# The waits of a three-bank PSUM ring rewritten, and two of its rounds moved to another phase, in a fused attention and mixture-of-experts kernel

## The chip, the cores and the metric

One core of a Trainium2 chip. The metric is the device time of one launch in microseconds (us), lower is better. Before the change it is 879.34 us, the median of three runs (878.54 to 879.36).

## What is computed

Two blocks, one after the other, in fp32 on `x` of 2 x 1024 rows of 256. Cut to what matters:

```python
# q from the layer-normed x (1024 rows), keys and values from 64 context rows and the same 1024 rows
q, k, v = map(to_heads, (q, k, v))            # 8 heads of 64, per batch of 2
q = l2norm(q) * q_scale
k = l2norm(k) * k_scale
sim = jnp.einsum('bhid,bhjd->bhij', q, k) * SCALE
sim = jnp.where(full_mask, sim, max_neg)      # the mask is over the 64 context keys
attn = jax.nn.softmax(sim.astype(jnp.float32), axis=-1)
out = jnp.einsum('bhij,bhjd->bhid', attn, v)
x = x + layer_norm(out @ Wo, ln_o_w, ln_o_b)
...
x = x + shared_swiglu(h) + top2_of_16_experts(h)   # h = layernorm(x)
```

The change touches the attention alone.

## The kernel before

**Stages.** Projections come first (to about 114 us), then attention, `stage_b(i)` for `PAIRS = 8` pairs `i` of one batch entry and two heads (114 to about 514 us), then the output projection, the shared experts and the routed experts. Each engine's program is written out by hand, and semaphores tie them; nothing is scheduled by a tool.

**A pair.** There are 1024 queries in `CH = 2` halves of 512, and `TK = 9` key tiles of 128. A *slot* (`score_slot`, L798 to L824) is one key tile against one half for both heads: three products (`L814`) and one that adds the negated row maxima (`L823`), eight matmuls into two of the banks 0 to 3. ScalarE turns each bank into `prob` (`exponentials`, L1145 to L1160, one instruction a head). A pair has 18 slots, in six *phases* `f` of three. After its three slots a phase *weighs* the three `prob` of the phase before, six matmuls (12 with both passes of fp32) into bank 7 (`weigh`, L826 to L842). In phases 0 and 3 a `total` (L844 to L850) follows: the row sums of one half, from `acc`, which GpSimd adds up out of `prob` (L634, L639). The last three `prob` of a half are added on VectorE (`add_tail`, L1401 to L1409) and put onto `acc` by GpSimd (L645).

**The maxima of the next pair.** While pair `i` runs, TensorE transposes the rows of pair `i+1` (`turn_heads`, phases 0 and 1) and makes 17 *rounds* (`piece_round`, L755 to L782). A round is one query tile against one half of the keys, two matmuls, one a head (`L768`); round 16 is the masked context keys (`L774`, `L779`, 18 small matmuls). VectorE reduces each of the two banks to row maxima (`reduce_round`, `L1361`, `L1364`), and after round 16 `negate` (`L1370`, `L1374`) makes `zneg`. The next pair's first matmul (`turn_neg`, `L788`) transposes it, and VectorE spreads it (`keep_neg`, `L1379`).

**Where a round stands.** `ROUNDS[f]` has four places: ahead of the phase's first slot, and behind each of its three slots. VectorE goes through the same lists, place by place (`stage_b`, L1456 on). In phase 3 it does `add_tail` first; in phases 2 and 5 a `divide` (`L1426`, it needs `rec`, which comes back by DMA) stands behind the rounds, and in phase 5 ahead of `negate`. Pair 0 makes its own rounds and those of pair 1 by other lists (`FIRST_ROUNDS`), which the change leaves alone, and pair 7 makes none.

**The ring.** Turns, rounds, `neg` and `sum` all write banks 4, 5, 6 in turn: use `u` of the list `ring_order` takes bank `4 + u % RING`, `RING = 3`, and must wait until use `u - 3` has been read. VectorE counts `ring_used` up for each of them but the sums, ScalarE counts `sum_kept` for the sums (`keep_sum`, L1162 to L1167). `ring_freed(n)` and `ring_kept(n)` are the two counts after `n` uses. Both heads of a round wait ahead of the round's first matmul:

```python
        def ring_slot(*key):

            u = ring_at[key]
            if u >= RING:
                wait(pe, ring_used, ring_freed(u + 1 - RING))
                wait(pe, sum_kept, ring_kept(u + 1 - RING))
            return ring_bank(u)
...
            two = [ring_slot("piece", i, r, h) for h in range(2)]
```

Round 13 of pair 1, as one of the others, has two: first the `ring_used` of its second head, then both `sum_kept`, and the matmul carries the `ring_used` of its first head.

Of the kernel before, what the change touches and what calls it, by code (L numbers as in the profile page):

```python
# [60 lines left out]
RING = 3  # L61
# [7 lines left out]
def wait(eng, sem, value):  # L69

    if isinstance(value, int) and value <= 0:
        return
    eng.wait_ge(sem, value)

def build(nc, x, ctx, mask, ln_x_w, ln_x_b, ln_l_w, ln_l_b, wq, wkv, q_scale, k_scale, wo,
# [6 lines left out]
    def sem(name):  # L83
        return es.enter_context(nc.semaphore(name))
# [143 lines left out]
    ring_made, ring_used, hi_ready = sem("ring_made"), sem("ring_used"), sem("hi_ready")  # L228
# [3 lines left out]
    sum_kept, o_kept, sum_spread = sem("sum_kept"), sem("o_kept"), sem("sum_spread")  # L232
# [31 lines left out]
    def slot_loop(eng, body):  # L264
# [6 lines left out]
        for s in range(NS // 4 * 4, NS + 1):  # L271
# [3 lines left out]
    MASKED_ROUND = CH * TQ  # L275
    K_LEFT, Q_LEFT, K_RIGHT, K_CTX, Q_RIGHT = range(TURNS)
    TURN_AT = {0: (K_LEFT, Q_LEFT), 1: (K_RIGHT, K_CTX, Q_RIGHT)}
    ROUNDS = {1: ((), (0,), (1,), (2,)), 2: ((3,), (4,), (5,), (6,)), 3: ((7,), (8,), (9,), (10,)),
              4: ((11,), (12,), (13,), (14,)), 5: ((15,), (16,), (), ())}

    HALF = TQ // CH
    LATE_MASKED = MASKED_ROUND + 1
# [15 lines left out]
    def phase_rounds(i, f):  # L298
# [3 lines left out]
        if i + 1 == PAIRS:  # L302
            return [()] * (BATCH + 1)
        return [[(i + 1, r) for r in place] for place in ROUNDS.get(f, ((),) * (BATCH + 1))]

    def masked_tiles(i, r):

        if i == 0:
            return {MASKED_ROUND: (0, HALF), LATE_MASKED: (HALF, TQ)}.get(r)
        return (0, TQ) if r == MASKED_ROUND else None  # L310
# [7 lines left out]
    ring_at, ring_order = {}, []  # L318
# [33 lines left out]
    def ring_freed(n):  # L352

        return sum(key[0] != "sum" for key in ring_order[:n])

    def ring_kept(n):

        return sum(key[0] == "sum" for key in ring_order[:max(n, 0)])

    def ring_bank(u):  # L360

        return bank[4 + u % RING]
# [324 lines left out]
    def _(pe):  # L687
# [46 lines left out]
        def ring_slot(*key):  # L734

            u = ring_at[key]
            if u >= RING:
                wait(pe, ring_used, ring_freed(u + 1 - RING))
                wait(pe, sum_kept, ring_kept(u + 1 - RING))
            return ring_bank(u)  # L740

        def turn_heads(i, g):

            b, j = divmod(i, PAIRS // B)
            cols = slice(j * P, (j + 1) * P)
            if g == K_CTX and b == 1 and j == 0:
                pe.wait_ge(k_used, NT + B)
            src, first, n = {K_LEFT: (kn, 0, 4), K_RIGHT: (kn, 4, 4), K_CTX: (kn, TQ, 1),
                             Q_LEFT: (on, 0, 4), Q_RIGHT: (on, 4, 4)}[g]
            dst = ring_slot("turn", i, g)  # L750
            for a in range(n):
                last = nc.tensor.transpose(dst[:, a * P:(a + 1) * P], src[:, first + a, b, cols], ident[:, :])  # L752
            last.then_inc(ring_made, 1)

        def piece_round(i, r):  # L755

            p, b = i % 2, i // (PAIRS // B)
            two = [ring_slot("piece", i, r, h) for h in range(2)]
            if masked_tiles(i, r) is None:
                t, c = divmod(r, CH)  # L760
                if r == 0:
                    pe.wait_ge(ring_used, ring_freed(ring_at[("turn", i, Q_LEFT)] + 1))
                if r == 1:
                    pe.wait_ge(ring_used, ring_freed(ring_at[("turn", i, K_RIGHT)] + 1))
                if t == TQ // 2 and c == 0:
                    pe.wait_ge(ring_used, ring_freed(ring_at[("turn", i, Q_RIGHT)] + 1))
                for h, rows in enumerate((LOW, HIGH)):
                    mm_(two[h][:, :], q_hi[p][rows, t * P:(t + 1) * P], k_hi[p][rows, c * QC:(c + 1) * QC],  # L768
                        start=True, stop=True).then_inc(ring_made, 1)
            else:  # L770
                t0, t1 = masked_tiles(i, r)
                pe.wait_ge(ring_used, ring_freed(ring_at[("turn", i, K_CTX if t1 <= TQ // 2 else Q_RIGHT)] + 1))
                for h, rows in enumerate((LOW, HIGH)):
                    mm_(two[h][:, 0:(t1 - t0) * M].rearrange("p (t m) -> p t m", m=M), firstrow[rows, :],  # L774
                        maskrow[rows, b, :].unsqueeze(1).to_broadcast([DH, t1 - t0, M]),
                        start=True, stop=False, skip_group_check=True)
                for t in range(t0, t1):
                    for h, rows in enumerate((LOW, HIGH)):
                        last = mm_(two[h][:, (t - t0) * M:(t - t0 + 1) * M], q_hi[p][rows, t * P:(t + 1) * P],  # L779
                                   k_hi[p][rows, S:S + M], start=False, stop=(t == t1 - 1), skip_group_check=True)  # L780
                        if t == t1 - 1:
                            last.then_inc(ring_made, 1)  # L782

        def turn_neg(i):

            dst = ring_slot("neg", i)
            pe.wait_ge(neg_ready, i + 2 if i else 1)
            nc.tensor.transpose(dst[:, 0:P], zneg[:, :, :].rearrange("p a d -> p (a d)"), ident[:, :])\  # L788
                .then_inc(ring_made, 1)
# [68 lines left out]
        project(bank[CTX_BANK[0][2]], NT, 0, 2)  # L858
        pe.wait_ge(k_used, NT)
        piece_round(0, 0)  # L860
        project(bank[CTX_BANK[1][1]], NT + 1, 1, 1)
        piece_round(0, 2)
        turn_heads(0, K_RIGHT)
        project(bank[CTX_BANK[1][2]], NT + 1, 1, 2)
        piece_round(0, 4)
        project_late(0)
        piece_round(0, 6)
# [854 lines left out]
```

## Time and profile before

| | |
|---|---|
| median of 3 runs | 879.34 us (878.54 to 879.36) |
| the profiled execution | 881.1 us, its span 879.4 us |
| mean granted TensorE clock | 0.987 of full speed |
| TensorE busy | 818.0 us (93%) |
| VectorE busy | 486.0 us (55%) |
| ScalarE busy | 343.0 us (39%) |
| GpSimd busy | 327.7 us (37%) |
| the chain that ended last | PE 78%, DVE 6%, issue 5%, POOL 4% |

The profile names TensorE PE (PEld is its weight load), VectorE DVE, ScalarE ACT, GpSimd POOL, and SyncE's DMA queue SPq. Lines such as L768 are lines of the kernel before. The ends of matmuls are modelled, and with an unbroken stream the next starts ahead of the modelled end of the last; starts are the better clock.

### The profile page before, as it was taken

The page shows a single profiled execution, that of the slowest core. Times are in us where ns is not written, and L with a number is a line of the kernel's source. Part 1 is how long each engine was busy: PE and PEld are TensorE (multiplying, and loading weights), DVE is VectorE, ACT ScalarE, POOL GpSimd, SP SyncE. Part 2 cuts the span into 40 slices and gives each one's busy share as a digit, 9 for nine tenths or more (in the row PEclk, how much of TensorE's full clock was granted, in tenths as well). Part 3 has the DMA queues.
Part 4 walks back from the last instruction along what each step waited for, and adds up shares of the span by engine and source line. Part 5 has one row for each costly group of instructions (what it writes and reads, how often), then busy time and mean ns, then how long its engine had stood idle before and what let it go on. Part 6 is the DMA issues. An engine that isn't in the chain of part 4 may idle for free.

```text
span 879.4 us, 13186 instructions
## 1 busy us (share of the span) xinstructions
PE 818.0 (93%) x4329; PEld 499.1 (57%) x4330; DVE 486.0 (55%) x904; ACT 343.0 (39%) x652; POOL 327.7 (37%) x250
## 2 busy tenths in 40 slices
PE   5999988999999999999999999999669999999996
PEld 2444354545545454545554446755336999998554
DVE  2887767766675757675672377656112433432442
ACT  2545354555646455655646321121001333333101
POOL 2100044366665555465666843302730000000670
PEclk9999999999999999999999999999979999999999
DMA  3015600000000000000002002590520232222440
GB/s 109 25 37 173 216 1 1 13 13 13 13 3 13 12 14 13 13 13 13 13 13 73 13 25 61 194 308 31 197 84 15 88 95 89 89 94 68 125 137 24
DMA packets 55253, 55.99 MB, mean 64 GB/s; under 512 B 11810, under 2 KB 50340, under 8 KB 55204
## 3 DMA queue, kind: packets, MB, share of 16 engines
q1 hardware_dynamic: 50980, 46.96, 17.0%
q0 software_dynamic: 3072, 8.39, 2.9%
q8 instruction: 29, 0.48, 0.2%
q10 hardware_dynamic: 1152, 0.00, 0.1%
q14 instruction: 20, 0.16, 0.1%
HBM read 36.60 MB, written 18.67 MB: 63 GB/s over the span
## 4 chain that ended last, share of the span: by engine, by line
PE 78%; DVE 6%; issue 5%; POOL 4%; another core or an unknown queue 2%; ACT 2%; DVEq 2%; DMA 1%; ACTq 0%; POOLq 0%
PE bank L840 11%; PE bank L705 10%; PE bank L983 10%; PE bank L814 10%; PE bank L1048 10%; PE bank L768 6%; PE bank L998 5%; PE bank L1057 5%; PE bank L823 3%; POOL acc L639 2%; PE bank L894 2%; PE bank L752 2%; PE bank L849 1%; PE bank L1038 1%
## 5 line engine op out<-in xcount | busy, mean ns | idle before, releaser
L1160 ACT ACTIVATE prob<-bank,zero 128x512 f32<-128x512 f32 x256 | 160.2, 687 | 127.0 <-PE bank L823 121.3
L1361 DVE TENSOR_REDUCE mx<-bank 128x1 f32<-128x512 f32 x256 | 164.9, 686 | 61.5 <-PE bank L768 59.1
L639 POOL TENSOR_TENSOR acc<-acc,prob 128x1024 f32<-128x1024 f32 x64 | 152.2, 2378 | 30.1 <-ACT prob L1160 23.0
L840 PE MATMUL bank<-prob,vn 128*64 128x512 f32 x576 | 134.2, 601 | 0.6 <-DVE on L1426 0.6
L983 PE MATMUL bank<-xfT,w12s 128*128 128x512 f32 x256 | 115.9, 598 | 1.8 <-DVE yn L1509 1.1
L681 POOL DMA_INDIRECT slot_result<-slot_results,posi x32 | 30.6, 956 | 176.8 <-DMA slot_results<-yo 163.1
L1048 PE MATMUL bank<-xsT,w_slot 128*128 128x128 f32 x752 | 91.9, 275 | 1.0 <-ACT xsT L1250 1.0
L1048 PEld LDWEIGHTS bank<-xsT,w_slot 128*128 128x128 f32 x752 | 89.2, 191 | 6.0 <-ACT xsT L1250 1.6
L998 PE MATMUL bank<-w3s,gsh 128*128 128x256 f32 x256 | 64.7, 397 | 17.5 <-DVE gsh L1493 17.5
L645 POOL TENSOR_TENSOR acc<-acc,tail 128x1024 f32<-128x1024 f32 x16 | 38.0, 2376 | 115.1 <-DVE tail L1409 115.1
L1240 ACT ACTIVATE sil<-bank 128x512 f32<-128x512 f32 x32 | 18.9, 597 | 156.3 <-PE bank L983 107.2
L983 PEld LDWEIGHTS bank<-xfT,w12s 128*128 128x128 f32 x256 | 49.1, 193 | 52.9 <-issue 49.5
L768 PE MATMUL bank<-k_hi,q_hi 64*128 64x512 f32 x256 | 63.7, 484 | 14.8 <-DVE mx L1361 9.6
L840 PEld LDWEIGHTS bank<-prob,vn 128*64 128x64 f32 x576 | 37.2, 136 | 69.2 <-issue 48.9
L768 PEld LDWEIGHTS bank<-k_hi,q_hi 64*128 64x128 f32 x256 | 26.6, 184 | 77.7 <-DVE mx L1361 47.5
L998 PEld LDWEIGHTS bank<-w3s,gsh 128*128 128x128 f32 x256 | 49.9, 199 | 35.2 <-DVE gsh L1493 19.6
L814 PE MATMUL bank<-q_hi,k_hi 64*128 64x512 f32 x288 | 63.5, 422 | 6.1 <-ACT prob L1160 6.1
L1493 DVE TENSOR_TENSOR gsh<-sil,bank 128x512 f32<-128x512 f32 x32 | 21.8, 685 | 75.1 <-ACT sil L1240 41.9
L823 PE MATMUL bank<-neg_max,ones_r 64*128 64x512 f32 x288 | 59.5, 393 | 0.0
L814 PE MATMUL bank<-q_lo,k_hi 64*128 64x512 f32 x288 | 59.4, 393 | 0.0
L814 PE MATMUL bank<-q_hi,k_lo 64*128 64x512 f32 x288 | 59.4, 392 | 0.0
L634 POOL TENSOR_TENSOR acc<-prob 128x1024 f32<-128x1024 f32 x16 | 37.8, 2364 | 52.9 <-ACT prob L1160 52.9
(161 smaller groups left out, 1088.1 us busy)
## 6 DMA issues: line engine op xcount, KB each, us to landing
w12r<-in_L_ffn_routed_w SPq DMA_DIRECT2D x32, 256.0 KB
slot_rows<-zrow SPq DMA_DIRECT2D x47, 128.0 KB, 1.9
xsl<-slot_rows SPq DMA_DIRECT2D x47, 128.0 KB, 2.0
slot_results<-yo SPq DMA_DIRECT2D x47, 128.0 KB, 1.7
w3r<-in_L_ffn_routed_w SPq DMA_DIRECT2D x16, 256.0 KB
rec<-row_sum_reciprocals SPq DMA_DIRECT2D x28, 128.0 KB, 2.9
xin<-in_x SPq DMA_DIRECT2D x16, 128.0 KB, 2.1
w12s<-in_L_ffn_shared_w SPq DMA_DIRECT2D x2, 1024.0 KB, 7.0
```

The lines of the kernel that those rows point to most:

```text
L639: g.tensor_tensor(acc[:, m % 2, :, :], acc[:, m % 2, :, :], prob[:, (n + kt) % PROBS, :, :], ALU.add).then_inc(summed, 1)
L705: last = mm_(dst[:, :], xT_of(n, c)[:, k, :], wqkv[:, k, j * INNER:(j + 1) * INNER], start=(k == 0), stop=(k == DK - 1))
L768: mm_(two[h][:, :], q_hi[p][rows, t * P:(t + 1) * P], k_hi[p][rows, c * QC:(c + 1) * QC], start=True, stop=True).then_inc(ring_made, 1)
L814: mm_(two[h][:, :], lhs[rows, keys], rhs[rows, queries], start=(lhs is k_hi[p] and rhs is q_hi[p]), stop=False)
L823: mm_(two[h][:, :], ones_r[rows, :], neg_max[rows, queries], start=False, stop=True)\
L840: last = mm_(bank[O_BANK][rows, :], vn[:, kt, b, (2 * j + h) * DH:(2 * j + h + 1) * DH], prob[:, n % PROBS, h, :], start=(kt == 0), stop=( ...
L983: last = mm_(bank[2 * (u % 2) + w][:, :], w12s[:, k, w, u * P:(u + 1) * P], xfT[:, k, bass.ds(g * GR, GR)], start=(k == 0), stop=(k == DK ...
L998: last = mm_(bank[4 + j // 2][:, (j % 2) * D:(j % 2 + 1) * D], gsh[:, u % 2, j * P:(j + 1) * P], w3s[:, u, :], start=(u == 0 and j % 2 == ...
L1048: last = mm_(bank[2 + p][:, j * P:(j + 1) * P], w_slot[:, p, k, j * P:(j + 1) * P], xsT[:, p, k, :], start=(k == 0), stop=(k == DK - 1))
L1057: last = mm_(bank[6 + p][:, 0:D], rgT[:, p, k * P:(k + 1) * P], w3r[:, e, k, :], start=(k == 0), stop=(k == HID // P - 1))
L1160: a(prob[:, n % PROBS, h, :], bank[2 * (n % 2) + h][:, :], ACT.Exp, bias=bias).then_inc(probs_ready, 1)
L1361: v.tensor_reduce(mx[:, h, t, c:c + 1], ring_bank(u)[:, :], AX.X, ALU.max).then_inc(ring_used, 1)
```

## The change

`ROUNDS` holds the rounds of phases 3, 4 and 5 two places later: rounds 7 and 8 alone are in phase 3, behind its second and third slot; phase 4 has 9 to 12, phase 5 has 13 to 16. Its lists are those of pairs 1 to 6. The rounds' waits are written by `ring_two`: a wait for `sum_kept` only where the bank's last use was a sum, and one wait for `ring_used`, at the second head's count. Turns, `neg` and sums wait for the one semaphore that their bank's last user counts.

```diff
-    ROUNDS = {1: ((), (0,), (1,), (2,)), 2: ((3,), (4,), (5,), (6,)), 3: ((7,), (8,), (9,), (10,)),
-              4: ((11,), (12,), (13,), (14,)), 5: ((15,), (16,), (), ())}
+    ROUNDS = {1: ((), (0,), (1,), (2,)), 2: ((3,), (4,), (5,), (6,)), 3: ((), (), (7,), (8,)),
+              4: ((9,), (10,), (11,), (12,)), 5: ((13,), (14,), (15,), (16,))}
...
             u = ring_at[key]
-            if u >= RING:
-                wait(pe, ring_used, ring_freed(u + 1 - RING))
-                wait(pe, sum_kept, ring_kept(u + 1 - RING))
+            old = u - RING
+            if old >= 0:
+                if ring_order[old][0] == "sum":
+                    pe.wait_ge(sum_kept, ring_kept(old + 1))
+                else:
+                    pe.wait_ge(ring_used, ring_freed(old + 1))
             return ring_bank(u)
+
+        def ring_two(i, r):
+
+            u = ring_at[("piece", i, r, 0)]
+            old = max(u - RING, 0), u + 1 - RING
+            for o in old:
+                if ring_order[o][0] == "sum":
+                    pe.wait_ge(sum_kept, ring_kept(o + 1))
+            if any(ring_order[o][0] != "sum" for o in old):
+                pe.wait_ge(ring_used, ring_freed(old[1] + 1))
+            return ring_bank(u), ring_bank(u + 1)
...
-            two = [ring_slot("piece", i, r, h) for h in range(2)]
+            two = ring_two(i, r)
```

**Place A: TensorE, phase 3 of pair 1, from its start to its third slot.** Before (L768 is a round, L814 with a wait on `probs_ready` the start of a slot):

```order
L768 MATMUL bank<-k_hi,q_hi 128x512 [waits ring_used,sum_kept]
L768 MATMUL bank<-k_hi,q_hi 128x512
L814 MATMUL bank<-q_hi,k_hi 128x512 [waits probs_ready]
...
L823 MATMUL bank<-neg_max,ones_r 128x512
L768 MATMUL bank<-k_hi,q_hi 128x512 [waits sum_kept,ring_used]
L768 MATMUL bank<-k_hi,q_hi 128x512
L814 MATMUL bank<-q_hi,k_hi 128x512 [waits probs_ready]
```

With the change (L782 is the round, L828 the slot):

```order
L828 MATMUL bank<-q_hi,k_hi 128x512 [waits probs_ready]
...
L837 MATMUL bank<-neg_max,ones_r 128x512
L828 MATMUL bank<-q_hi,k_hi 128x512 [waits probs_ready]
...
L837 MATMUL bank<-neg_max,ones_r 128x512 x2
L782 MATMUL bank<-k_hi,q_hi 128x512 [waits ring_used]
L782 MATMUL bank<-k_hi,q_hi 128x512
L828 MATMUL bank<-q_hi,k_hi 128x512 [waits probs_ready]
```

The phase opens with two slots and no round, and the first round of the phase stands behind the second slot, with one wait.

**Place B: VectorE, from the tail add of pair 1's phase 3 to the negation** (`tail` is phase 3's add, `spread_rec` ends phase 4, `on` is the `divide` of phase 5). Before:

```order
L1409 TENSOR_TENSOR tail<-tail,prob 128x1024 [waits probs_ready]
L1361 TENSOR_REDUCE mx<-bank 128x1 [waits ring_made] x16
L1433 RECIPROCAL spread_rec<-spread 128x8 [waits rec_stored,sum_spread]
L1361 TENSOR_REDUCE mx<-bank 128x1 [waits ring_made] x2
L1364 TENSOR_REDUCE mx<-bank 128x8 [waits ring_made] x2
L1426 TENSOR_TENSOR on<-o_raw,rec 128x4x128 [waits o_kept,rec_loaded]
L1370 TENSOR_REDUCE mm<-mx 128x16
L1374 TENSOR_SCALAR zneg<-mm 128x2x8 [waits ring_made]
```

With the change:

```order
L1423 TENSOR_TENSOR tail<-tail,prob 128x1024 [waits probs_ready]
L1375 TENSOR_REDUCE mx<-bank 128x1 [waits ring_made] x12
L1447 RECIPROCAL spread_rec<-spread 128x8 [waits rec_stored,sum_spread]
L1375 TENSOR_REDUCE mx<-bank 128x1 [waits ring_made] x6
L1378 TENSOR_REDUCE mx<-bank 128x8 [waits ring_made] x2
L1440 TENSOR_TENSOR on<-o_raw,rec 128x4x128 [waits o_kept,rec_loaded]
L1384 TENSOR_REDUCE mm<-mx 128x16
L1388 TENSOR_SCALAR zneg<-mm 128x2x8 [waits ring_made]
```

Four reduces, two rounds, have moved from behind the tail add to phase 5, ahead of the `divide` and the negation.

## Rows read from the trace of the kernel before

**Rows 1.** The page, busy time of the engines: us (share of the span) x instructions.

```profile
PE 818.0 (93%) x4329; PEld 499.1 (57%) x4330; DVE 486.0 (55%) x904; ACT 343.0 (39%) x652; POOL 327.7 (37%) x250
```

**Rows 2.** The page, costliest groups: busy us, mean ns | idle before, and its releaser.

```profile
L1361 DVE TENSOR_REDUCE mx<-bank 128x1 f32<-128x512 f32 x256 | 164.9, 686 | 61.5 <-PE bank L768 59.1
L768 PEld LDWEIGHTS bank<-k_hi,q_hi 64*128 64x128 f32 x256 | 26.6, 184 | 77.7 <-DVE mx L1361 47.5
```

**Rows 3.** Timeline of TensorE, phase 2 of pair 2: start, us, what [idle before].

```profile
237.44 0.50 PE L768 MATMUL bank<-k_hi,q_hi 64*128 64x512 f32 x2
...
238.92 0.50 PE L768 MATMUL bank<-k_hi,q_hi 64*128 64x512 f32 x2
...
241.86 0.51 PE L768 MATMUL bank<-k_hi,q_hi 64*128 64x512 f32 x2
242.30 2.80 PE L840 MATMUL bank<-prob,vn 128*64 128x512 f32 x12
245.02 0.50 PE L768 MATMUL bank<-k_hi,q_hi 64*128 64x512 f32 x2
```

**Rows 4.** Timeline of VectorE, the same phase.

```profile
237.98 1.29 DVE L1361 TENSOR_REDUCE mx<-bank 128x1 f32<-128x512 f32 x2 [1.79 <-PE bank L768]
239.43 1.29 DVE L1361 TENSOR_REDUCE mx<-bank 128x1 f32<-128x512 f32 x2 [0.16 <-PE bank L768]
```

**Rows 5.** Timeline of TensorE, phase 0 of pair 0, before any sum.

```profile
116.99 0.50 PE L768 MATMUL bank<-k_hi,q_hi 64*128 64x512 f32 x2 [1.65 <-DVE q_lo L1351]
...
121.02 0.50 PE L768 MATMUL bank<-k_hi,q_hi 64*128 64x512 f32 x2
```

**Rows 6.** Timeline of VectorE, the same phase.

```profile
117.50 5.31 DVE L1361 TENSOR_REDUCE mx<-bank 128x1 f32<-128x512 f32 x8 [0.65 <-PE bank L768]
```

**Rows 7.** Timeline of VectorE, phase 3 of pair 2: the reduces behind the tail add.

```profile
246.61 2.68 DVE L1361 TENSOR_REDUCE mx<-bank 128x1 f32<-128x512 f32 x4
```

**Rows 8.** Timeline of TensorE, phases 3 to 5 of pair 2, to the next pair.

```profile
247.50 0.50 PE L768 MATMUL bank<-k_hi,q_hi 64*128 64x512 f32 x2 [1.05 <-DVE mx L1361]
...
250.83 2.79 PE L840 MATMUL bank<-prob,vn 128*64 128x512 f32 x12
...
254.42 0.50 PE L768 MATMUL bank<-k_hi,q_hi 64*128 64x512 f32 x2
...
262.05 0.49 PE L768 MATMUL bank<-k_hi,q_hi 64*128 64x512 f32 x2
...
269.37 0.33 PE L788 MATMUL bank<-ident,zneg 128*128 128x128 f32 x1
```

**Rows 9.** Timeline of TensorE, phase 0 of pair 2: the starts of its three slots.

```profile
221.45 0.50 PE L814 MATMUL bank<-q_hi,k_hi 64*128 64x512 f32 x2
...
222.48 0.39 PE L814 MATMUL bank<-q_hi,k_hi 64*128 64x512 f32 x2
...
224.08 0.50 PE L814 MATMUL bank<-q_hi,k_hi 64*128 64x512 f32 x2 [0.51 <-ACT prob L1160]
```

**Rows 10.** Timeline of TensorE, round 16 of pair 1 at pair 0's end.

```profile
167.37 0.50 PE L774 MATMUL bank<-maskrow,firstrow 64*128 64x512 f32 x2
...
168.62 2.79 PE L840 MATMUL bank<-prob,vn 128*64 128x512 f32 x12
171.34 0.33 PE L788 MATMUL bank<-ident,zneg 128*128 128x128 f32 x1
```

**Rows 11.** Timeline of VectorE, the same place.

```profile
169.89 0.68 DVE L1426 TENSOR_TENSOR on<-o_raw,rec 128x512 f32<-128x512 f32 x1
...
170.94 0.17 DVE L1374 TENSOR_SCALAR zneg<-mm 128x16 f32<-128x16 f32 x1
```

**Rows 12.** Timeline of GpSimd, the tail's addition in phase 3 of pair 2.

```profile
246.77 2.37 POOL L645 TENSOR_TENSOR acc<-acc,tail 128x1024 f32<-128x1024 f32 x1 [6.48 <-DVE tail L1409]
```

**Rows 13.** Timeline of SyncE's queue, phase 5 of pair 2.

```profile
262.27 1.09 SPq L476 DMA_DIRECT2D rec<-row_sum_reciprocals  x2
```

**Rows 14.** The page, DMA issues: KB each, median us from issue to landing.

```profile
rec<-row_sum_reciprocals SPq DMA_DIRECT2D x28, 128.0 KB, 2.9
```

## The prediction

> **What bounds the kernel now.** The page first: TensorE is busy 93% of the span, the others 37 to 55% [rows 1]. So nothing but TensorE's own path can pay, and only where it stands still or waits. The costliest groups then name a pair that wait for each other: the reduces of the rounds (L1361) idle 61.5 us ahead of themselves, 59.1 of it on a round's matmul, and the weight loads of those matmuls stand 77.7 us, 47.5 of it on that reduce [rows 2]. That is a loop through the three-bank ring, and the timeline shows its pace. In phase 2 of pair 2 the four rounds start at 237.44, 238.92, ... 241.86, three intervals in 4.42 us or 1.47 each [rows 3], and VectorE starts a pair of reduces 1.45 after the last, 1.29 of work and 0.16 of idling [rows 4]. Round r+1 needs the bank that the first reduce of round r frees. VectorE could be faster: in phase 0 of pair 0, where no sum has been in the ring and a round has one wait instruction instead of two, eight reduces run on end in 5.31 us, 1.33 a round [rows 6], and four rounds start in 121.02 - 116.99 = 4.03 us [rows 5]. It is the same arithmetic with no idle between the reduces.
>
> By phases of pair 2: phase 2 is 7.58 us (237.44 to 245.02) [rows 3], phase 3 is 254.42 - 245.02 = 9.40, phase 4 is 7.63, phase 5 is 7.32 [rows 3, 8]. Phase 3 is long because VectorE does the tail adds ahead of its rounds: its reduces begin at 246.61, two rounds back to back [rows 7], so round 8 goes only at 247.50, where TensorE has idled 1.05 us [rows 8].
>
> **The change, part by part.** No matmul, reduce or DMA is added or removed; six pairs (1 to 6) have their rounds moved, and all waits are rewritten.
>
> *The waits.* Between the reduce that binds and the round's first matmul stood one more wait instruction (the two `sum_kept`) and, since the second head's wait came first, the matmul's own. Now the matmul itself carries the wait that binds. With one such instruction fewer the loop already keeps up with VectorE [rows 5, 6]; with none left the floor is still VectorE's 1.33. So I take 4.03 us for the three intervals of a full phase, in place of 4.42: 0.39. Bounds of that: nothing (the difference has another cause), and below, since a faster reaction also starts the first round after a reduce sooner, perhaps 0.1 more a phase, as much as the one wait instruction did per interval (1.45 less 1.33 is 0.12). I take the middle because the nearest row has no instruction fewer than VectorE allows.
>
> The Trainium skill, page "Advanced Engine Details and Errata" (Network/Comms), gives 50 to 100 ns for a sequencer's reading of a semaphore. By that, as an estimate, an interval would gain 0.05 to 0.10 instead of 0.12 to 0.13, and the wait part some 4 to 7 us; the rows of pair 0 speak for more.
>
> Phase 1 has two such intervals, 2 x 0.12 = 0.24. Phase 2: 0.39. Phase 4: its rounds took until the weighing as in phase 2, 0.05 more since a sum stands between; now 4.03, then 0.44 from the last round to the weighing [rows 3], then 2.72 of weighing (242.30 to 245.02), 7.19 against 7.63: 0.44. Phase 0 is as before: its slots wait for ScalarE [rows 9].
>
> *Phase 3, two rounds fewer.* It opens with two slots on end. Phase 0 shows such slots: starts at 0, 1.03 and 2.63 us, the third held 0.51 us by ScalarE's `prob` [rows 9]. Round 7 takes about 0.3 and falls into those 0.51, so it costs nothing; were ScalarE not late there, it would cost 0.3. VectorE is free of the tail at 1.6 us into the phase (246.61 - 245.02), before round 7 is made at about 2.3, so the tail no longer stands on TensorE's path. Round 8 follows the third slot at 2.63 + 1.03 = 3.66, and the bank it needs is free, since round 7's first reduce is over by 3.4. Then 0.44 to the weighing, and 254.42 - 250.83 = 3.59 for weighing and total [rows 8]: 7.69 in place of 9.40, a gain of 1.71. The total needs `acc` with the tail: GpSimd starts that 0.07 behind the tail and takes 2.37, to 249.14, 4.1 us into the phase [rows 12]; the total is wanted at 6.7. It is covered, with 2.6 us to spare where 4.3 were.
>
> *Phase 5, two rounds more.* Pair 0's last phase has exactly this form (three rounds, then the masked one behind the third slot): from the masked round to the weighing 1.25 us, then 2.72 to `L788` [rows 10]. So 4.03 + 1.25 + 2.72 = 8.00 in place of 7.32: a loss of 0.68. What is late next is the negation: `zneg` must be there when the weighing ends. In pair 0 it ends at 171.11 with the `divide` ahead of it, and `L788` starts at 171.34 without idling [rows 10, 11]; the margin is 0.23 us, and I take the stall as nothing. The bounds are nothing and 0.4 a pair, should an instruction of that chain slip.
>
> Sum: a pair gains 0.24 + 0.39 + 1.71 + 0.44 - 0.68 = 2.10 us, six pairs 12.6. Pair 0 makes pair 1's rounds with the long waits from phase 4 on, seven intervals at 0.12: 0.8. Pair 7 has no rounds. In all **13.4 us**, 881.1 to 867.7 for the profiled execution. The median of the runs is 1.8 below that, so 879.3 to **865.9**. All that follows the attention starts from its last phases, so it moves up with it; I cost its shift at nothing. Of the 13.4 the waits alone would be about 9.9 and the moved rounds, with the old waits, (1.71 - (4.42 + 3.97 - 7.32)) x 6 = 3.8.
>
> **The rivals.**
>
> *The waits gain nothing.* Pair 0's faster pace could come from something else that differs there. For it: one sample of the clean kind. Against: VectorE's 0.16 of idling [rows 4] is the same in every round behind the first sum and absent ahead of it [rows 6]. Only the moved rounds are left, 3.8 us: 875.5. Chance 0.08.
>
> *The moved rounds gain nothing* because round 7 behind the second slot holds up the third, or VectorE turns out late there. The waits remain, about 9.9 us: 869.4. Against: TensorE idles 0.51 in that place [rows 9]. Chance 0.07.
>
> *VectorE's floor is higher.* The Trainium skill, page "VectorE: DVE Perf Modes" (The DRAIN you can't avoid), says that the next operation does not start until the pipe of the last is empty. As a mechanism here: the 686 ns of a reduce [rows 2] would be the step, 1.37 a round and not 1.33. With eleven intervals a pair that gives back 11 x 0.04 x 6 + 0.3, or 2.9 us: 868.8. The trace disagrees, with 5.31 us for eight where 8 x 0.686 is 5.49 [rows 2, 6]. Chance 0.02.
>
> *Slower: the `divide` holds the negation.* It stands ahead of `negate` in phase 5 and needs `rec`, a DMA of 2.9 us [rows 14] issued at 262.27 to 263.4 [rows 13], landed by about 266.3, 11.9 us after phase 4's start. The `divide` comes about 13.8 us after that start now. Each us by which the DMA is late beyond that stops TensorE, since `L788` heads its queue and the whole next pair stands behind. It decides from 1.9 us late on, and turns the change into a loss from 13.4 / 6 = 2.2 us more; at 5 us late it would be 881. Nothing shows such a landing. Chance 0.03.
>
> *It doesn't do what it says.* Were a wait left in, or the removed ones already folded by the builder, the time would be that of the second or first rival or 879. The order rows show one semaphore where there were two. Chance of no change 0.03.
>
> **How the numbers follow.** The forecast has 0.77 and its own spread: 0.1 a phase more from a quicker reaction in four phases of six pairs and pair 0 is about 2.8 us further down, 863; a stall of 0.4 at each pair's end is 2.4 up, 868.3. The range reaches to the two nearest rivals, 868.8 and 869.4, and leaves out 875.5 and the slower case: **862.5 to 871**. About 0.2%, 1.8 us, is what a measurement of this kernel can tell from no change. Faster by more than that: 0.77 + 0.08 + 0.07 + 0.02 = 0.94; the same 0.03; slower 0.03.
>
> **What would show it.** Right: round intervals of 1.33 to 1.35 in phases 2, 4 and 5 with VectorE's 0.16 of idling gone; phase 3 of about 7.7 us with no wait on `mx` in it; phase 5 of about 8.0 and no idling on `zneg` ahead of `L788`; phases 2 to 5 of a pair 30.1 us in place of 31.9. Wrong: intervals still 1.45 (the waits gain nothing); phase 3 above 9 us (a new wait at round 7 or 8); an idle of TensorE on `zneg`; any stretch of the attention past pair 0 with the granted clock at its lower level.

## The result, and the profile after

| | before | after |
|---|---|---|
| median | 879.35 us (878.54 to 879.77, 4 runs) | 860.64 us (860.18 to 861.0, 4 runs) |
| ratio | | 0.9784, interval 0.9769 to 0.9798 |
| span of the profiled execution | 879.4 us | 858.8 us |

The change gains 18.7 us, 2.2%. The forecast was 13.4 us and 865.9; the range ended at 862.5, 1.9 above the result. The sign and the mechanism held, the size did not.

The page after: busy times, the group that answers to the first of [rows 2], and the slots' first matmuls with what holds them:

```profile
PE 805.9 (94%) x4329; PEld 490.4 (57%) x4330; DVE 486.3 (57%) x904; ACT 342.3 (40%) x652; POOL 327.9 (38%) x250
...
L1375 DVE TENSOR_REDUCE mx<-bank 128x1 f32<-128x512 f32 x256 | 164.4, 686 | 54.5 <-PE bank L782 54.1
...
L828 PE MATMUL bank<-q_hi,k_hi 64*128 64x512 f32 x288 | 63.1, 432 | 8.1 <-ACT prob L1174 8.0
```

The work is the same to the instruction. TensorE's busy time fell by 12.1 us all the same, presumably because its modelled ends cover short waits; so starts are compared here, not busy times. From one `neg` matmul (L788 before, L802 now) to the next:

| us | pair 0 | 1 | 2 | 3 | 4 | 5 | 6 |
|---|---|---|---|---|---|---|---|
| before | 56.71 | 48.98 | 49.05 | 48.97 | 49.04 | 49.10 | 49.02 |
| after | 53.56 | 46.08 | 46.71 | 46.08 | 46.11 | 46.12 | 46.12 |

Pairs 1 to 6 give 294.16 - 277.22 = 16.9 us. Pair 0 gives 3.15, some 1.6 of it no part of the change: in the profiled execution before, TensorE was granted half its clock for about 3 us of pair 0, and in the one after it was not. Here the two windows before, then after (columns: window, length, busy us and count of PE, PEld, DVE, ACT, POOL, granted clock, DMA share, GB/s):

```profile
136.00:138.00 2.00, 2.00 (x11) 1.51 (x12) 0.69 (x1) 0.70 (x2) 0.00 (x0) 0.50 0.00 0
138.00:140.00 2.00, 2.00 (x14) 1.34 (x10) 1.29 (x2) 1.27 (x3) 0.00 (x0) 0.69 0.00 0
```

```profile
136.00:138.00 2.00, 2.00 (x20) 1.45 (x16) 1.33 (x3) 1.39 (x3) 0.00 (x0) 1.00 0.00 0
138.00:140.00 2.00, 2.00 (x10) 0.64 (x12) 2.00 (x4) 1.35 (x3) 0.00 (x0) 1.00 0.00 0
```

The loss is 2 x 0.50 + 2 x 0.31 = 1.6 us, as an estimate. The same dip stands in pair 0 of some of the other traces and not of others: the changed kernel, run again, has none and takes 53.52 us for pair 0, and with a settled wait ahead (a kernel below, whose pairs are no longer) it has one and takes 54.87. It would explain most of the 1.8 us by which the profiled execution before stood above its median. So 16.9 + 1.5 = 18.4 of the 18.7 us lie in the attention's pairs 0 to 6.

The timeline of TensorE after, phases 2 to 5 of pair 2, answers to [rows 3, 8]:

```profile
230.96 0.50 PE L782 MATMUL bank<-k_hi,q_hi 64*128 64x512 f32 x2
...
232.24 0.50 PE L782 MATMUL bank<-k_hi,q_hi 64*128 64x512 f32 x2
...
234.87 0.43 PE L782 MATMUL bank<-k_hi,q_hi 64*128 64x512 f32 x2
235.23 2.80 PE L854 MATMUL bank<-prob,vn 128*64 128x512 f32 x12
237.96 0.50 PE L828 MATMUL bank<-q_hi,k_hi 64*128 64x512 f32 x2
...
240.87 0.49 PE L828 MATMUL bank<-q_hi,k_hi 64*128 64x512 f32 x2 [0.55 <-ACT prob L1174]
...
245.81 0.50 PE L782 MATMUL bank<-k_hi,q_hi 64*128 64x512 f32 x2
...
260.99 0.30 PE L802 MATMUL bank<-ident,zneg 128*128 128x128 f32 x1 [0.24 <-DVE zneg L1388]
```

Rounds start 1.28 us apart (232.24 - 230.96), the whole phase's four in 3.91. Phase 3 is 245.81 - 237.96 = 7.85, its third slot held by ScalarE and no round held by `mx`. VectorE in phase 2, against [rows 4]:

```profile
231.49 5.14 DVE L1375 TENSOR_REDUCE mx<-bank 128x1 f32<-128x512 f32 x8 [1.75 <-PE bank L782]
```

Eight reduces in 5.14 us where the "run on end" of [rows 6] took 5.31: that row was not VectorE's limit. Pair 2 takes 46.71 us, the others 46.08 to 46.12. Two things differ in it. Where it ends, TensorE idles 0.24 us on `zneg`, which it does in no other pair. And in phase 3 it waits 0.55 us for `prob`, where it waits 0.27 in each of the other five, because ScalarE starts the phase's first `prob` 0.28 us later (pair 2, then pair 3, whose phases 3 start at 237.96 and 284.63):

```profile
239.55 2.42 ACT L1174 ACTIVATE prob<-bank,zero 128x512 f32<-128x512 f32 x4 [3.14 <-PE bank L837]
285.94 2.42 ACT L1174 ACTIVATE prob<-bank,zero 128x512 f32<-128x512 f32 x4 [2.87 <-PE bank L837]
```

### The profile page after: what moved, and what is told of

It reads as the page before. It is cut to its first block, busy times and chain, and to the rows that moved or that the text cites. A ratio compares the mean times of both kernels' runs of the same rounds, so it can differ in the third digit from the quotient of the medians.

```text
span 858.8 us, 12948 instructions
## 1 busy us (share of the span) xinstructions
PE 805.9 (94%) x4329; PEld 490.4 (57%) x4330; DVE 486.3 (57%) x904; ACT 342.3 (40%) x652; POOL 327.9 (38%) x250
## 4 chain that ended last, share of the span: by engine, by line
PE 80%; issue 5%; POOL 4%; DVE 4%; ACT 3%; another core or an unknown queue 2%; DVEq 1%; DMA 1%; ACTq 0%; POOLq 0%
PE bank L854 12%; PE bank L705 10%; PE bank L997 10%; PE bank L828 10%; PE bank L1062 10%; PE bank L1012 6%; PE bank L782 5%; PE bank L1071 5%; PE bank L837 3%; POOL acc L639 2%; ACT prob L1174 2%; PE bank L908 2%; PE bank L766 2%; PE bank L863 1%
## 5 line engine op out<-in xcount | busy, mean ns | idle before, releaser
L828 PE MATMUL bank<-q_hi,k_hi 64*128 64x512 f32 x288 | 63.1, 432 | 8.1 <-ACT prob L1174 8.0
L782 PE MATMUL bank<-k_hi,q_hi 64*128 64x512 f32 x256 | 62.1, 481 | 5.7 <-DVE mx L1375 2.0
L837 PE MATMUL bank<-neg_max,ones_r 64*128 64x512 f32 x288 | 57.4, 392 | 0.0
L828 PE MATMUL bank<-q_hi,k_lo 64*128 64x512 f32 x288 | 57.2, 390 | 0.0
L828 PE MATMUL bank<-q_lo,k_hi 64*128 64x512 f32 x288 | 57.1, 390 | 0.0
L1673 DVE TENSOR_TENSOR rgT<-sil,bank 128x256 f32<-128x256 f32 x47 | 19.8, 422 | 65.2 <-ACT sil L1269 65.2
L705 PE MATMUL bank<-wqkv,xT 128*128 128x512 f32 x112 | 52.3, 616 | 3.2 <-ACT xT L1105 3.2
```

Of the source, the lines that this page charges most:

```text
L705: last = mm_(dst[:, :], xT_of(n, c)[:, k, :], wqkv[:, k, j * INNER:(j + 1) * INNER], start=(k == 0), stop=(k == DK - 1))
L828: mm_(two[h][:, :], lhs[rows, keys], rhs[rows, queries], start=(lhs is k_hi[p] and rhs is q_hi[p]), stop=False)
L837: mm_(two[h][:, :], ones_r[rows, :], neg_max[rows, queries], start=False, stop=True)\
```

## The experiments

There are three groups of four kernels, each with the kernel before beside them. The first group (waits only to half reduces) ran on one chip (number 6), beside a kernel before of 879.15 us (877.58 to 880.97). The second (one ahead, one behind, "two behind", three rounds) and the third (two steps, a wait a head, after again, three rounds again) ran on another (number 3), beside 857.52 (855.59 to 858.33) and 857.56 (855.47 to 859.01). The same kernel is 22 us faster on chip 3, in the stages after the attention: between 600 and 660 us of after's first trace TensorE was busy 44.7 us of 60 at a granted clock of 0.86, and between 580 and 640 us of the later trace 59.0 us at 1.00. What makes the two chips differ there no run shows. Pairs 1 to 6 of the changed kernel have the same length in its first trace and in the one from chip 3, to 0.05 us each, so kernels are compared on the same chip, or by ratio, and by their pairs.

### The two parts alone

The new waits with the old `ROUNDS`, and the old waits with the new `ROUNDS`.

> The new waits with the old table of rounds. Theory M (the reaction behind the binding wait was the loop's slack, and with one wait on the matmul TensorE itself sets 1.28 us a round): round intervals 1.28 in phases 2 and 4, phase 3 about 9.0 and phase 5 about 7.1, a pair about 46.9 us, 865 us in all, so the waits alone bring 14.3 of the 18.7. Theory V (VectorE's floor of 1.33, as predicted): intervals 1.33 and about 869.5.

> The old waits with the new table of rounds. Theory M: intervals stay 1.45, phase 3 about 7.8 against 9.4, phase 5 about 8.4 against 7.3, a gain of 0.5 a pair: about 876 us. The prediction's sum for this part alone was 875.5. If most of the gain that the forecast missed came from the moved rounds, this is below 872.

| | median | ratio | pairs 1 to 6 | mean interval, phase 2 |
|---|---|---|---|---|
| waits only | 863.43 (862.19 to 864.97) | 0.9813 (0.9797 to 0.9829) | 46.81 to 46.86 | 1.30 |
| rounds only | 875.32 (874.58 to 876.24) | 0.995 (0.9934 to 0.9967) | 48.07 to 48.22, pair 2 48.69 | 1.47 |

The moved rounds alone gain 3.8 us, to the tenth what the forecast had for them. The waits alone gain 15.7 where it had 9.9. The parts add up (19.5) to a little more than the whole (18.7). The phases came close to these expectations: with the waits alone phase 3 takes 8.93 and phase 5 7.2 us, with the rounds alone 7.57 (7.84 in pair 2) and 8.3. Pair 2's longer pair comes with the moved rounds, whatever the waits. With old waits VectorE still idles 0.16 ahead of each pair of reduces:

```profile
233.24 1.29 DVE L1361 TENSOR_REDUCE mx<-bank 128x1 f32<-128x512 f32 x2 [0.16 <-PE bank L768]
```

### Shorter reduces

Is the loop VectorE's floor or the reaction to it? In the changed kernel and in the kernel before, the maxima of plain rounds are taken over 256 of the 512 columns. What is left out is half of each bank's maximum.

```diff
-  v.tensor_reduce(mx[...], ring_bank(u)[:, :], AX.X, ALU.max)
+  v.tensor_reduce(mx[...], ring_bank(u)[:, 0:QC // 2], AX.X, ALU.max)
```

> The changed kernel, with each of VectorE's row maxima taken over 256 of a bank's 512 columns (the other half is left out), so that VectorE's work in a round falls by about half a us. Theory M: TensorE sets the interval, it stays 1.27 to 1.28, and only ends of chains gain: 859 to 861 us. Theory V (VectorE sets it): intervals fall well below 1.28 and the time to about 845.

> The kernel before, with the same halved row maxima (256 of 512 columns). Theory M: the loop through VectorE was what made 1.45 to 1.47, so the interval falls to TensorE's own 1.28 although the waits are the old ones: 12 to 15 us less than before, 865 to 867. Were the wait instructions themselves costly on TensorE, whatever VectorE does, the interval would stay near 1.4 and the time above 872.

In the changed kernel: 857.27 us (856.74 to 858.61), ratio 0.975, pairs 45.76 to 45.84 with pair 2 at 46.4. VectorE, with 0.76 us in place of 1.29 for a round, now idles 0.4 and more between rounds, and the slot behind the third round waits for ScalarE, as TensorE's weight load shows:

```profile
231.85 0.76 DVE L1375 TENSOR_REDUCE mx<-bank 128x1 f32<-128x256 f32 x2 [0.42 <-PE bank L782]
...
233.02 0.18 PEld L828 LDWEIGHTS bank<-q_hi,k_hi 64*128 64x128 f32 x2 [0.48 <-ACT prob L1174]
```

And yet the four rounds of a phase take 3.91 us as in after. The intervals are 1.28, 1.15 and 1.48: a slot and a round together occupy TensorE for 1.15, then the last slot comes late. So at 1.28 the changed kernel is some 0.3 us a pair from what an almost free VectorE would give; the bound has passed to the pace of ScalarE's `prob` and TensorE itself. The time is 2 us below the 859 to 861 that I expected.

In the kernel before, with its old waits: 856.85 us (856.45 to 857.7), ratio 0.9741, pairs 45.68 to 45.72. This missed its expectation by 8 us or more. I had expected a rest of the old waits' cost to stay. None did: with 0.53 us taken out of VectorE's side of the loop the loop closes in time with the old waits too, and phase 3 falls from 9.40 to 8.10, because the reduces behind the tail add are shorter. The wait instructions still stand there, and behind a reduce that binds a round still starts as late as in the kernel before (0.226 us, see below). They cost something only while they are in the loop that binds.

### Where the binding wait stands

```diff
+            pe.wait_ge(masks_made, 1)        # one behind
+            pe.wait_ge(ident_made, 1)        # two behind: this one as well
             two = ring_two(i, r)
+            pe.wait_ge(masks_made, 1)        # one ahead: this one alone
```

> The changed kernel with one more wait, long satisfied, in an instruction AHEAD of each round's matmul, which still carries the wait that binds. Position theory: it is passed while the ring is still held, intervals stay 1.28, 860 to 861.5 us. Count theory (every wait instruction costs about 0.1 wherever it stands): 90 rounds after pair 0's start, 8 us more, 868.

> The changed kernel with the binding wait moved to a wait instruction of its own and a long satisfied wait on the matmul, as the rounds of pair 0 had it in the kernel before: one step behind the binding wait. Position theory: intervals 1.34, 0.06 for 11 intervals a pair in six pairs and those of pair 0, about 5 us: 865 to 866. Count theory: as e5, 868.

> The changed kernel with two steps behind the binding wait: the binding wait in one instruction, a satisfied one in the next, a satisfied one on the matmul, as the kernel before had it behind the first sum. Position theory: intervals 1.45 as before, and the whole gain of the waits is gone: about 875, as e2_rounds_only. Count theory: 16 us more, 876; only e5 and e6 tell these apart.

The third did not become what its text says: in plain rounds the ring's wait and one of the others share one instruction, so that it is still one step ahead of the matmul. Only the rounds with a further wait (0, 1, 8 and 16) have it two steps ahead. The next kernel has three such waits, two called ahead of `ring_two` and one (`w_loaded`) behind it, and its plain rounds are `[ring_used]`, `[projections_loaded, ident_made]`, matmul with `masks_made` (`projections_loaded` at 64 is how the program names the wait on `w_loaded`).

```diff
+            pe.wait_ge(masks_made, 1)
+            pe.wait_ge(ident_made, 1)
             two = ring_two(i, r)
+            pe.wait_ge(w_loaded, 16 * 2 * DK)
```

> The changed kernel with three waits that always hold (masks, identity, weights) called beside the ring's wait in every round, so that in the built program the wait that binds stands in a wait instruction two steps ahead of the first scores matmul, as in the rounds of phases 2 to 5 of the kernel before. If the place of the binding wait alone sets the interval between rounds, it goes from 1.28 to about 1.45 us, the pairs from 46.1 to about 48.2, and the time is about 14 us above the changed kernel's (12 to 15). If the number of steps does not matter beyond the first (the one-behind kernel's 1.33 to 1.36), the interval stays at about 1.35 and the time is 6 us above the changed kernel's; then the rest of the old interval came from the wait for the second head's bank, which the kernel before had ahead of the first head's matmul.

> The changed kernel again, for the comparison of the others of this call on the same chip: ratio to the kernel before 0.976 to 0.979, pairs 46.1 to 46.7 us.

| ring's wait, plain rounds | kernel | ratio | pairs but 2 | mean interval, phase 2 |
|---|---|---|---|---|
| on the matmul | after, again | 0.9782 (0.9768 to 0.9797) | 46.06 to 46.11 | 1.30 |
| on the matmul, a settled wait ahead | one ahead | 0.9765 (0.975 to 0.978) | 46.02 to 46.09 | 1.30 |
| one instruction ahead | one behind | 0.9829 (0.9813 to 0.9845) | 46.73 to 46.76 | 1.35 |
| one ahead, shared | "two behind" | 0.9881 (0.9866 to 0.9896) | 47.18 to 47.26 | 1.35 |
| two ahead | two steps | 0.9967 (0.9956 to 0.9978) | 48.08 to 48.18 | 1.46 |
| two ahead | rounds only | 0.995 (0.9934 to 0.9967) | 48.07 to 48.22 | 1.47 |

The medians are 838.75 (after, again), 837.34, 843.39, 847.09 and 854.25 us on chip 3, in the table's order; rounds only ran on chip 6. The kernel with two steps has the new `ring_two` and nothing of the old waits but their place, and it is 15.5 us slower than after on its chip, where the new waits, added to the new rounds, had gained 14.7 (875.32 to 860.64). Its pairs 1 to 6 equal those of the old waits with the new rounds. It is a little slower than that kernel, by 1.5 us in ratio, and pair 0 shows where: 58.16 against 56.71 us, since the rounds of pair 0 before the first sum had one step in the kernel before and have two in this one. Its VectorE shows the same 0.16 [rows 4]:

```profile
234.94 1.29 DVE L1378 TENSOR_REDUCE mx<-bank 128x1 f32<-128x512 f32 x2 [0.17 <-PE bank L785]
```

The kernel with one step gives back the row that the forecast had read as VectorE on end [rows 6]:

```profile
234.28 5.31 DVE L1376 TENSOR_REDUCE mx<-bank 128x1 f32<-128x512 f32 x8 [1.78 <-PE bank L783]
```

The traces also show the step by itself. From the recorded end of the reduce that frees the second head's bank to the start of the round's first weight load it takes, in 44 to 54 rounds of pairs 1 to 6 of each trace (most of the others are the first behind another piece of work):

| steps | kernels | us | interval |
|---|---|---|---|
| none | after, one ahead | 0.052 to 0.054 | 1.28 |
| one | one behind | 0.115 to 0.116 | 1.34 |
| two | before, rounds only, two steps | 0.225 to 0.227 | 1.45 |

This settles the cause. It is neither the number of semaphores nor the number of wait instructions (the one-ahead kernel has one more in every round and its pairs are no longer; it has as many in TensorE's trace as the one-behind kernel, 341 each, against 241 of after), but how many steps the sequencer still has to take between the event and the matmul: 0.06 us for the first and 0.11 for the second, in the reaction as in the interval. By the means of phase 2 it is 0.05 for one step and 0.16 for two, since the last interval of a phase is 1.35 in after too: there the slot waits for ScalarE, and its weight load starts at 233.83 in pair 2, 0.05 us behind the end of ScalarE's second `prob`. The "two behind" kernel agrees round by round. It costs 0.48 us a pair over the one-behind kernel with the same plain intervals, and its pair 3 shows where: round 0 comes 0.19 us later after `neg` (11.16 against 10.97), round 1 then 1.45 after it and not 1.29, round 16 1.46 after round 15 and not 1.30. Those are three of the four rounds in which it does stand two steps away; round 8, the fourth, follows a slot that ScalarE holds.

### What is left: three rounds in phase 3, and one wait a head

Round 9 goes back to phase 3, so that phase 5 has three; the second kernel adds to this that each head's matmul of a plain round waits for its own bank.

```diff
-  3: ((), (), (7,), (8,)), 4: ((9,), (10,), (11,), (12,)), 5: ((13,), (14,), (15,), (16,))
+  3: ((), (7,), (8,), (9,)), 4: ((10,), (11,), (12,), (13,)), 5: ((14,), (15,), (16,), ())
```

```diff
-            two = ring_two(i, r)
+            plain = masked_tiles(i, r) is None
+            two = None if plain else ring_two(i, r)
...
-                    mm_(two[h][:, :], q_hi[p][rows, ...
+                    mm_(ring_slot("piece", i, r, h)[:, :], q_hi[p][rows, ...
```

> A version that may beat both: the changed kernel with three rounds in phase 3 (7, 8, 9 behind its three slots), 10 to 13 in phase 4, 14, 15 and the masked 16 in phase 5, one place earlier. In phase 3 the third slot waits 0.3 to 0.55 us for ScalarE, which hides a round; phase 5 loses one of 0.34 and the negation comes earlier. Theory M: phase 3 +0.1 to +0.2, phase 5 -0.34 and its occasional 0.24 stall gone: 0.15 to 0.4 a pair, 858 to 859.7. If the tail add holds round 7 or 8 up, phase 3 grows by more than 0.4 and it is slower than 861.

> The three-rounds kernel again beside the changed kernel: with 0.2 us a pair less and without the stall in pair 2 it should be 1 to 2.5 us below the changed kernel. If the two agree within 0.5 us, the difference seen between pairs is given back elsewhere.

> The three-rounds table, and in rounds without a mask each head's scores matmul waits for its own bank alone. The changed kernel waits for the later of the two banks ahead of the first head. If VectorE's reduce of the second bank is what the interval of 1.28 us ends on, head 0 can start some 0.6 us sooner and the interval falls towards VectorE's own floor (about 1.22): up to 0.06 x 17 x 6 = 6 us less. If ScalarE and TensorE's own work pace it (the half-reduce kernel gained only 0.3 us a pair), it gains 0 to 1.5 us over the three-rounds kernel. If the split breaks the two heads' matmuls apart (they run side by side in two halves of the array in the kernel before), each round costs TensorE more, by up to one matmul's 0.23 us, and it is slower than the three-rounds kernel by some us.

| | median | ratio | pairs 1 to 6 |
|---|---|---|---|
| after, again | 838.75 (837.97 to 839.35) | 0.9782 (0.9768 to 0.9797) | 46.06 to 46.11, pair 2 46.71 |
| three rounds | 837.03 (835.88 to 837.37) | 0.9756 (0.9743 to 0.977) | 45.90 to 45.93, pair 2 46.12 |
| three rounds, again | 836.66 (836.51 to 837.11) | 0.9758 (0.9743 to 0.9772) | 45.88 to 45.91, pair 2 46.12 |
| and a wait a head | 833.49 (832.9 to 833.67) | 0.9718 (0.9704 to 0.9733) | 45.44 to 45.47, pair 2 45.75 |

Both beat the changed kernel on the same chip, the first by 2.1 us and the second by 5.3. In the first phase 3 is 0.08 us longer than in after and phase 5 0.28 shorter, and TensorE no longer waits for `zneg` in pair 2. The second's gain over the first, 3.2 us, lies above the 0 to 1.5 that I took as likeliest and below the 6 of VectorE's floor; its pairs show 0.43 in the mean, 2.6 in six. Its first head goes as soon as its own bank is free, and the intervals of phase 2 are 1.26, 1.16 and 1.47, those of the halved reduces, with the same sum of 3.9 as in after; what it gains lies in all of phases 1 to 5, 0.05 to 0.11 in each. What holds TensorE longest in the attention is ScalarE (who waits for whom: us in total, times, longest):

```profile
PE bank L829 <- ACT prob L1175: 6.1, 12, 0.5
```

Now VectorE does run on end, and its own step shows in phase 3:

```profile
238.67 2.48 DVE L1376 TENSOR_REDUCE mx<-bank 128x1 f32<-128x512 f32 x4
```

Two reduces are 1.29 and four are 2.48: the third and fourth add 1.19 together, 0.60 each. The same follows within one round: a pair takes 1.29 where one alone is recorded as 0.69. In the 5.31 of [rows 6], 0.69 and four steps of 0.60 inside the rounds leave 2.22 for the three starts between rounds, 0.74 each: 0.14 of waiting in each, which the row merges away. (The single records have 0.73, and between the recorded ends and starts 0.05 of idling, too little for the row to be parted.)

## Why the prediction was wrong in size, step by step

**The failed step** is "with none left the floor is still VectorE's 1.33", taken from [rows 5, 6], and the sentence behind it that the nearest row "has no instruction fewer than VectorE allows". Those rows were a loop with one step in it, so close to VectorE's own pace that the trace drew eight reduces as one run. VectorE's own round is about 1.20, and with the last step gone the loop closed at 1.28, or 1.30 as the mean of a phase. The tables show it: 1.46, 1.35 and 1.30 for two steps, one and none, or 1.45, 1.34 and 1.28 for the plain intervals. What VectorE can do could have been read before the change: two reduces take 1.29 [rows 4] and one is recorded as 0.69 [rows 2], so the second starts 0.60 behind the first, and eight on end would be 0.69 + 7 x 0.60 = 4.89 us and not 5.31. I had allowed for "a quicker reaction" of 0.1 a phase as the low end of the range; the reaction was there, in intervals as well as in first rounds, and about twice that.

The terms, for a pair (before: pair 2, whose pairs vary by 0.1; after: pair 1, which is like the later ones):

| | forecast gain | measured | |
|---|---|---|---|
| phase 1 | 0.24 | 8.65 - 8.18 = 0.47 | intervals and a first round's reaction |
| phase 2 | 0.39 | 7.58 - 6.99 = 0.59 | rounds 3.91, not 4.03; 0.37 to the weighing, not 0.44 |
| phase 3 | 1.71 | 9.40 - 7.57 = 1.83 | 7.85 in pair 2 |
| phase 4 | 0.44 | 7.63 - 7.07 = 0.56 | as phase 2 |
| phase 5 | -0.68 | 7.32 - 7.80 = -0.48 | 8.12 in pair 2, with the `zneg` stall |
| sum | 2.10 | 2.97 | the mean over six pairs is 2.82 |

2.82 x 6 = 16.9 against 12.6, and 1.5 against 0.8 in pair 0. The waits alone, 15.7 against 9.9, carry all of the miss. (The forecast doesn't work its 9.9 out; its terms with the new rounds give (0.24 + 0.39 + 0.44 + 0.39) x 6 + 0.8 = 9.6, against a measured 14.7.)

**What held.** The waits are in the binding loop of each round, so they pay at every interval. The moved rounds: 3.8 us forecast and 3.8 measured, with the slot held by ScalarE covering round 7, no wait on `mx` in phase 3, and `acc` not late for the total. Phase 5 is 0.2 better than pair 0's form because its three intervals shrank too. The low margin at `zneg` was named; it stalled in one pair by 0.24, less than the 0.4 of the bound. That the moved rounds came out to the tenth is luck: with the old waits the six pairs of the trace are 294.16 - 289.46 = 4.7 us shorter, and only the medians, whose ranges are 1.7 and 3.4 us wide, have 3.8. By the same count the waits alone bring 13.1 us in the six pairs.

**The rivals.** "The waits gain nothing" and "the moved rounds gain nothing" are excluded by the two parts run alone. "It doesn't do what it says" is excluded by the intervals. "VectorE's floor is higher", at 1.37 a round, fell the wrong way: with a step of 0.60 against a recorded duration of 0.686, the next reduce starts some 0.09 us ahead of the recorded end of the last. So a wait until the pipe of the last is empty, as the Trainium skill (page "VectorE: DVE Perf Modes", The DRAIN you can't avoid) has it, is not seen between recorded ends here; the same passage adds that an operation that is not held starts earlier. Whether the record runs past the emptying of the pipe no run shows. The slower case, a late `rec`, did not come: the `divide` starts at once behind the masked reduces in pair 2.

```profile
258.06 1.29 DVE L1378 TENSOR_REDUCE mx<-bank 128x8 f32<-128x512 f32 x2 [0.80 <-PE bank L793]
259.27 0.68 DVE L1440 TENSOR_TENSOR on<-o_raw,rec 128x512 f32<-128x512 f32 x1
260.04 0.20 DVE L1384 TENSOR_REDUCE mm<-mx 128x16 f32<-128x48 f32 x1
260.67 0.18 DVE L1388 TENSOR_SCALAR zneg<-mm 128x16 f32<-128x16 f32 x1 [0.43 <-issue]
```

One half of what makes pair 2 differ is the 0.43 of "issue" ahead of `zneg`. Of the nine `zneg` of the program it is the only one; in pair 3 `mm` starts at 306.43 and `zneg` at 306.71. The kernel before has the same 0.43 in the same pair (`mm` at 266.78, `zneg` at 267.41), 1.8 us ahead of its need, where it costs nothing. Moving work to the end of the phase brought it onto the path. The other half is ScalarE's late first `prob` in phase 3, which the kernel before has too (0.40 us behind the recorded end of its matmul, 0.12 in the other pairs) and hides behind the wait on `mx`. All fourteen traces have both pauses, at the same two instructions of the program. In each of them an 8 KB packet of an instruction queue starts 0.64 to 0.97 us after the instruction that comes late; the page of after counts twenty such packets:

```profile
q14 instruction: 20, 0.16, 0.1%
```

That would fit an engine that is short of instructions there. Others of these packets stand beside no pause, and no run moved one, so the cause stays open.

The price that the forecast set beside its own, 50 to 100 ns for a sequencer's reading of a semaphore (the Trainium skill, "Advanced Engine Details and Errata", Network/Comms), fits the runs in size: one step costs 0.06 us and the second 0.11. Used for both steps that were removed, and not for one, it would have given, as an estimate, 0.10 to 0.20 an interval, with the measured 0.16 inside.

## What to carry to other kernels

In a tight loop between two engines, count the steps that the sequencer takes after the event that comes last: put that wait on the instruction itself, and the long-settled ones ahead of it, where they cost nothing measurable. Split a wait that covers two instructions, so that each waits for what it alone needs, if what it frees is on the path. A row of merged instructions without idle is no proof that its engine is the limit: divide by the step that the engine shows inside a batch (here 0.60 us, not the recorded 0.69), and look for a place where it truly has work queued. Such a loop stops paying once the next engine paces it, which shortening the suspected engine's work shows in one run.

## What the runs showed of the hardware that was not expected

- A satisfied wait in a wait instruction ahead of the binding one is free on TensorE (pairs 46.02 to 46.09 with it, 46.06 to 46.11 without); behind the binding one it delays the weight load: 0.053 us from the reduce's end with no step, 0.115 with one, 0.226 with two.
- VectorE starts back-to-back PSUM reduces of 128x512 fp32 every 0.60 us, though each is recorded as 0.69; with 128x256 a pair takes 0.76.
- A round's two matmuls overlap (two in 0.50 us, where one is recorded at 0.48 in the mean). With a wait of its own for each the pair became 0.43 us shorter, not longer.
- The same kernel before ran at 879.15 us on one chip and at 857.5 on another, with the changed kernel's pairs 1 to 6 equal to 0.05 us between its first trace and the one from the second chip; the 22 us lay behind the attention.
- In pair 2 VectorE and ScalarE each start one instruction late (by 0.35 and 0.28 us), the same two in all fourteen traces, each time with an 8 KB packet of an instruction queue 0.64 to 0.97 us later.
